# Attention inside a fused AdaLN-attention-MoE kernel: values stationary, row sums on VectorE, softmax in halves, paired merges, first loads reordered

## The reference

```python
# _L0_cond_ref: one 256x256 matrix and bias for each sequence, picked by its category
c = einsum('bsi,bij->bsj', x, weight[ids]) + bias[ids][:, None, :]
# _L0_attn_ref: 16 heads of 16; every projection is W plus a low-rank product
Q, K, V = lora_linear(c, ...)
scores = einsum('bqhd,bkhd->bhqk', Q, K) / sqrt(16) + slopes * rel
out = einsum('bhqk,bkhd->bqhd', softmax(scores, axis=-1), V)
x = x + (c + rezero * lora_linear(out, Wo, bo, Ao, Bo))
# _L0_cond2_ref: low-rank product by language; _L0_ffn_ref: a shared GEGLU layer and
# 12 experts, of which each token takes two, weighted by a softmax over their two logits
x = x + shared(xf) + routed(xf)
```

## Time and profile before

| | us |
|---|---|
| median of 3 runs (range) | 844.94 (844.64 to 846.51) |
| profiled execution | 845.6 |
| its span, first to last instruction | 843.5 |
| PE busy / VectorE busy / ScalarE busy / GpSimd busy | 811.8 / 546.8 / 282.0 / 406.1 |
| granted TensorE clock, mean | 0.992 |

### The profile page before, as it was taken

The page is one execution under the profiler, slowest core; times in us unless marked ns, Lnnn a source line. Parts: engine busy times, 40 slices in busy tenths (PEclk is TensorE's granted clock), DMA queues, the critical chain, the costliest instruction groups (busy, mean ns, idle before and its releaser), DMA issues. The chain is left out here.

```text
span 843.5 us, 27449 instructions
## 1 busy us (share of the span) xinstructions
PE 811.8 (96%) x9371; PEld 675.0 (80%) x9372; DVE 546.8 (65%) x1231; ACT 282.0 (33%) x783; POOL 406.1 (48%) x511
## 2 busy tenths in 40 slices
PE   6899999999999999979999999999999999999995
PEld 5778888888888888856777888888888888888884
DVE  2586666666666667758887567676676666666662
ACT  0333333333333333433332333232323333332330
POOL 2133333444334444210101277777777777777762
PEclk9999999999999999999999999999999999999998
DMA  9445555555555553103863323222232323232222
GB/s 277 130 137 173 171 161 156 157 167 156 160 168 154 153 158 90 46 2 139 251 209 125 125 34 39 35 35 37 33 39 32 39 33 39 33 38 34 35 34 25
DMA packets 49004, 85.59 MB, mean 101 GB/s; under 512 B 7266, under 2 KB 27554, under 8 KB 48834
## 3 DMA queue, kind: packets, MB, share of 16 engines
q1 hardware_dynamic: 33634, 68.76, 26.2%
q0 software_dynamic: 13888, 15.13, 13.4%
q10 hardware_dynamic: 1440, 1.16, 0.5%
HBM read 68.48 MB, written 16.55 MB: 101 GB/s over the span
## 5 line engine op out<-in xcount | busy, mean ns | idle before, releaser
L1429 PE MATMUL ps<-arena,stage 128*128 x900 | 206.6, 379 | 0.0
L1429 PEld LDWEIGHTS ps<-arena,stage 128*128 128x128 f32 x900 | 165.3, 190 | 19.4
L480 POOL DMA_INDIRECT out_dram<-stage,to_row x75 | 120.6, 1608 | 74.9 <-DVE stage L1040 63.4
L636 ACT ACTIVATE stage<-ps 128x384 f32<-128x384 f32 x150 | 65.4, 488 | 241.6 <-PE ps L1416 241.6
L1416 PE MATMUL ps<-token_rows,token_rows_T 64*128 64x128 f32 x1800 | 129.2, 272 | 0.0
L1416 PEld LDWEIGHTS ps<-token_rows,token_rows_T 64*128 64x128 f32 x1800 | 118.8, 189 | 1.7
L472 POOL DMA_INDIRECT token_rows<-gated_rows,from_row x75 | 75.0, 1000 | 64.6 <-DVE to_row L923 42.0
L388 POOL TENSOR_TENSOR arena<-arena 128x256 f32<-128x256 f32 x32 | 23.3, 729 | 148.7 <-DVE arena L764 148.7
L1014 DVE COPY token_rows<-ps 128x128 f32<-128x128 f32 x75 | 21.8, 291 | 109.6 <-PE ps L1398 109.6
L1024 DVE TENSOR_TENSOR stage<-ps,stage 128x384 f32<-128x384 f32 x150 | 75.8, 547 | 1.8 <-ACT stage L636 1.8
L735 DVE TENSOR_REDUCE arena<-ps 128x16 f32<-128x1024 f32 x32 | 39.2, 1224 | 49.4 <-PE ps L1167 49.2
(11 more groups left out here) (170 smaller groups left out, 1482.1 us busy)
## 6 DMA issues: line engine op xcount, KB each, us to landing
stage<-in_we_dram SPq DMA_DIRECT2D x36, 512.0 KB, 4.2
arena<-in_cond_w_dram SPq DMA_DIRECT2D x64, 256.0 KB, 2.9
arena<-in_we_dram SPq DMA_DIRECT2D x12, 768.0 KB, 4.9
arena<-in_x_both_dram SPq DMA_DIRECT2D x32, 256.0 KB, 2.6
arena<-in_L_cond_bias_dram SPq DMA_DIRECT2D x64, 64.0 KB, 2.7
out_dram<-arena SPq DMA_DIRECT2D x32, 128.0 KB, 1.7
be_bc<-in_be_rows_dram SPq DMA_DIRECT2D x13, 192.0 KB, 2.7
gated_rows<-token_rows POOLq DMA_DIRECT2D x2, 1152.0 KB, 10.2
```

The lines of the kernel that those rows point to most:

```text
L480: pool.indirect_dma_start(out_rows, bass.IndirectOffsetOnAxis(to_row[:, t:t + 1], 0), y_sb[t % YR], None, compute_op=ALU.add).then_inc(d_a ...
L636: nc.scalar.activation(g_sb[hf].rearrange("p (j n) -> p j n", n=P), first_out[1][:, :, hf, :], ACT.Gelu).then_inc(g_ok, 1)
L1429: last = mm(ps[:, 4 + s % 2, 0:D], actT_sb[s % 2][:, hf, j * P:(j + 1) * P], arena[:, ds(e * E2 + (NJ * hf + j) * D, D)], start=(hf == 0 a ...
```

## The change

- `attend`: V is stationary (`vD` of 32 columns, without ones) and the transposed probabilities move, 64 columns. Each product lands in one of four column groups (32 partitions) of bank 7, already transposed: head dimension on partitions, queries along the row. It comes after `condition`, and in a tile with a merge between its weights and its biases.
- The row sums are a VectorE reduction over the 1024 probabilities (`sums`), inverted by `invert`, spread to 16 columns a head by ScalarE (`inverse_wide`), transposed by PE in the next tile (`inverse_transpose`), copied by ScalarE (`invT_copy`). `normalize(i-1)`, one multiplication, stands between the halves of `shift(i)`. The score no longer waits for `o_sb`.
- `shift` and the exponential work on halves of 512 columns, and the first four transposes of probabilities wait for the first half alone.
- Merges 0 and 1 of an expert run together at the end of the odd tile (`merge_pair`): weights fill bank 6, biases go to bank 7. ScalarE copies the biases at once (`pair_bias_copy`) and the weights in the next tile (`pair_copy`, 512 columns). In that next tile `low_rank` comes after the projections, and PE waits for `pair_bias` before `inverse_transpose`. SyncE loads stages 0 and 1 after one wait. The waits on merge counts are renumbered.
- First loads: x of tile 0 in two halves, `consts` in two parts (identity and `kmask` first), `ali_f` on SyncE's queue, the other constants behind, awaited under three semaphores; both category values are read before the four condition loads; tile 1 is loaded before Wo. The projection order becomes K, Q, V, O. VectorE adds c and the weights before the language constants, which move into tile 0 (`lang_setup`) and behind it; `router_rows` moves into tile 0, `router_products` behind it, and eight warm matmuls stand after `condition(0)`.

The core of the diff (removed lines are those of the kernel above):

```diff
+        near_loads = [(bo_bc, a["bo_rows"]), (bv_half, a["bv_half"])]
+        rest_loads = [
+            (ba[:, :, :].rearrange("p c n -> p (c n)"), a["lora_ba"]), (consts[:, EARLY:], a["consts"][:, EARLY:]),
+            (lang_i[:, :], a["lang_of"]), (lang_b[:, :], a["lang_rows"]),
+            (a_rows, a["lora_a"]), (aT.rearrange("p c l n -> p (c l n)"), a["lora_aT"])]
+        FIRST, NEAR, REST = 16 * 2, 16 * (len(near_loads) + 1), 16 * len(rest_loads)
+        PROJECTIONS = (1, 0, 2, 3)
...
+            sp.dma_start(x_in[0][:, D:2 * D], a["x_both"][0, :, D:2 * D]).then_inc(d_x[0], 16)
+            sp.dma_start(wm[PROJECTIONS[0]].rearrange("p c n -> p (c n)"), a["wT"][PROJECTIONS[0]]
+                         ).then_inc(d_wT[PROJECTIONS[0]], 16)
             sp.wait_ge(d_cat, 16)
             load_condition(0, 0)
...
             def exps(i):
...
+                for half in range(2):
+                    act.wait_ge(shift_sb, 2 * i + (half + 1))
+                    part = probs[:, 512 * half:512 * half + 512]
+                    nc.scalar.activation(part, part, ACT.Exp).then_inc(prob_sb, 1)
...
+            def inverse_wide(i):
+                act.wait_ge(inv_sb, i + 1)
+                if not isinstance(i, int) or i > 0:
+                    act.wait_ge(invT_ps, i)
+                for m in range(KC):
+                    heads = inverse.rearrange("p (g m h) -> p m g h", m=KC, h=2)[:, m]
+                    last = copy(inv_wide[:, m * P:(m + 1) * P].rearrange("p (g h d) -> p g h d", h=2, d=HD),
+                                heads.unsqueeze(3).to_broadcast([P, 4, 2, HD]))
+                last.then_inc(wide_sb, 1)
+            def invT_copy(i):
+                act.wait_ge(invT_ps, i + 1)
+                if not isinstance(i, int) or i > 0:
+                    act.wait_ge(o_sb, i)
+                copy(inv_T, ps[:, 7, D:2 * D]).then_inc(invT_sb, 1)
...
                 if not isinstance(i, int) or i > 0:
                     dve.wait_ge(pT_ps, 2 * i)
...
+                    dve.wait_ge(rsum_sb, i)
+                for half in range(2):
+                    banks = slice(2 * half, 2 * half + 2)
+                    top = smax[:, 8 * half:8 * half + 8].rearrange("p (g h) -> p g h", g=2)
+                    V.tensor_reduce(top, scores[:, banks], AX.X, ALU.max).then_inc(max_sb, 1)
+                    dve.wait_ge(max_sb, 2 * i + (half + 1))
+                    V.tensor_tensor(probs[:, 512 * half:512 * half + 512].rearrange("p (g h k) -> p g h k", g=2, k=S),
+                                    scores[:, banks], top.unsqueeze(3).to_broadcast([P, 2, 4, S]),
+                                    ALU.subtract).then_inc(shift_sb, 1)
...
+            def sums(i):
+                dve.wait_ge(prob_sb, 2 * i + 2)
+                if not isinstance(i, int) or i > 0:
+                    dve.wait_ge(inv_sb, i)
+                V.tensor_reduce(rsum, probs.rearrange("p (a k) -> p a k", k=S), AX.X, ALU.add).then_inc(rsum_sb, 1)
+            def invert(i):
+                dve.wait_ge(rsum_sb, i + 1)
+                if not isinstance(i, int) or i > 0:
+                    dve.wait_ge(wide_sb, i)
+                V.reciprocal(inverse, rsum).then_inc(inv_sb, 1)
             def normalize(i):
                 dve.wait_ge(o_ps, i + 1)
...
+                dve.wait_ge(invT_sb, i + 1)
+                if not isinstance(i, int) or i > 0:
+                    dve.wait_ge(att_ps, i)
+                V.tensor_tensor(oT.rearrange("p c n -> p (c n)"), ps[:, 7, 0:D], inv_T, ALU.mult).then_inc(o_sb, 1)
...
+            def lang_setup():
+                low_rank_weight(3, PROJECTIONS[3])
+                dve.wait_ge(d_rest, REST)
+                V.tensor_copy(tri_b[:, :], col["tri"]).then_inc(s_const, 1)
+                V.tensor_copy(lang_tmp, lang_b[:, :])
+                link(V.tensor_copy(lang_f, lang_i[:, :]))
+                for lang in range(NLANG):
+                    ins = V.tensor_scalar(lang_hot[:, :, lang], lang_f, float(lang), None, ALU.is_equal)
+                ins.then_inc(s_hot, 1)
+                dve.wait_ge(s_hot, 1)
+                lang_routers()
+            def tile_steps(i, odd, between=lambda: None):
                 shift(i)
                 if one_more:
                     k_spread(i + 1)
+                between()
                 if not isinstance(i, int) or i > 1:
                     t_mask(i - 2)
                 if not isinstance(i, int) or i > 0:
                     x2_add(i - 1, not odd)
                 pT_copy(i)
+                sums(i)
                 if one_more:
                     v_spread(i + 1, not odd)
+                invert(i)
                 if not isinstance(i, int) or i > 1:
                     logit_sum(i - 2)
...
                 if two_more:
                     c_add(i + 2, odd)
+            low_rank_weight(0, PROJECTIONS[0])
             c_add(0, False)
...
+            low_rank_weight(1, PROJECTIONS[1])
+            dve.wait_ge(d_first, FIRST)
+            V.tensor_scalar(bq_quarter, bq_col, 0.25, None, ALU.mult).then_inc(s_first, 1)
             k_spread(0)
+            low_rank_weight(2, PROJECTIONS[2])
+            dve.wait_ge(d_near, NEAR)
+            V.tensor_copy(ali, ali_f).then_inc(s_const, 1)
+            V.tensor_scalar(bo_rz, bo_bc, rz, None, ALU.mult).then_inc(s_first, 1)
+            dve.wait_ge(s_zero, 3)
             v_spread(0, False)
             c_add(1, True)
...
+            tile_steps(0, False, lang_setup)
             router_consts()
+            link(V.tensor_scalar(lang_tmp, lang_tmp, col["lang_row"], col["one_row"], ALU.is_equal, ALU.add))
+            for hf in range(2):
+                V.tensor_scalar(langB[:, hf, :], lang_tmp, col["half"][:, hf:hf + 1], None, ALU.mult)
...
             def prob_transpose(i):
...
+                    if n % 4 == 0:
+                        pe.wait_ge(prob_sb, 2 * i + (n // 4 + 1))
...
             def attend(i, odd):
...
+                if not isinstance(i, int) or i > 0:
+                    pe.wait_ge(x2T_sb, i)
+                for m in range(KC):
+                    for b in range(2):
+                        for g in range(4):
+                            last = mm(ps[32 * g:32 * g + 32, 7, m * P + b * S:m * P + (b + 1) * S],
+                                      vD[int(odd)][:, b, 4 * m + g, :], probsT[:, 2 * g + m, b * S:(b + 1) * S],
                                       start=True, stop=True)
                 last.then_inc(o_ps, 1)
...
+            def inverse_transpose(i):
+                pe.wait_ge(wide_sb, i + 1)
+                for c in range(KC):
+                    last = tr(ps[:, 7, D + c * P:D + (c + 1) * P], inv_wide[:, c * P:(c + 1) * P], ident)
+                last.then_inc(invT_ps, 1)
+            def output(i):
                 pe.wait_ge(o_sb, i + 1)
...
             def merge(n, j, arrived, rows, inside):
...
+                merge_weights(j, 0)
+                inside()
+                merge_biases(j, 6, CW).then_inc(merge_ps, 1)
+            def merge_pair(e, i, inside):
+                for j in range(2):
+                    pe.wait_ge(d_stage[j], 16 * e + 32)
+                pe.wait_ge(tT_sb, i - 1)
+                pe.wait_ge(merge_sb, 2 * e + 2)
+                pe.wait_ge(x2T_sb, i)
+                for j in range(2):
+                    merge_weights(j, j * CW)
+                inside()
+                for j in range(2):
+                    last = merge_biases(j, 7, D + j * P)
...
+            def tile_steps(i, odd, merged, single=None, pair=None, after_pair=None,
+                           between=lambda: None):
...
                 score(i)
                 if one_more:
                     c_transpose(i + 1)
...
+                if after_pair is not None:
+                    pe.wait_ge(pair_bias, after_pair + 1)
+                if not isinstance(i, int) or i > 0:
+                    inverse_transpose(i - 1)
+                if late and after_pair is None:
                     low_rank(i - 2, merged)
                 if one_more:
                     project_k(i + 1)
                     project_q(i + 1)
...
+                if late and after_pair is not None:
                     low_rank(i - 2, merged)
+                between()
                 if not isinstance(i, int) or i > 0:
                     output(i - 1)
                 prob_transpose(i)
...
                     x2_transpose(i - 1, not odd)
                 if one_more:
                     project_v(i + 1)
...
                 if two_more:
                     condition(i + 2, odd)
...
+                if single:
+                    merge(*single, rows=i - 1 if late else None, inside=lambda: attend(i, odd))
+                elif pair is not None:
+                    merge_pair(pair, i, inside=lambda: attend(i, odd))
+                else:
+                    attend(i, odd)
             condition(0, False)
+            warm(8)
+            pe.wait_ge(d_first, FIRST)
             c_transpose(0)
```

(35 more changed lines are left out.)

209 lines of the change are left out of this document (74 added, 135 removed).

## The result

The changed kernel takes **825.2 us** (median; 824.58 to 825.74) against 845.04 of the kernel before on the same chip: a ratio of 0.9758, 95% interval 0.9743 to 0.9773. One further execution took 2746.6 us and is left out; nothing here explains it. The profiled execution took 824.58, with a span of 822.7 (before 843.5) and a mean clock of 0.994.

What follows compares the result with a forecast made beforehand. TensorE was taken to bound the attention stage, VectorE's softmax close behind. From 845.6 us: start -6.3, merge pairs -7.1, tiles 27 to 29 -0.4, tile 30 -0.8, tile 3 +0.9 gave 831.9, as a median 831; range 820 to 842.

Steps and rivals of the forecast that it cites:

- The start: Loads and setup before tile 1: first score at 18.0 to 18.5 us against 25.83, 6.3 us gained after tile 0's payback.
- Attend: Its 32 passes in each tile would take 0.60 us instead of 0.99, saving 0.38 a tile (0.2 to 0.48).
- The chain to x2: VectorE's operations up to `x2_add`: TensorE would newly idle 0.44 us before the x2 transposes, starting at T + 5.84.
- Of the halves nothing is left: Softmax halves: x2 transposes would still come 0.2 us later than before in merge tiles, 0.3 later in the others.
- Even and odd tile: Merge tiles: even 10.32 us against 10.50, odd 11.40 against 11.81, 0.59 a pair, times 12: 7.1 us.
- Late tiles: Tiles 27 to 29, after the merges: 8.9 us each against 9.05, 0.4 us gained in all.
- Tile 30: The tile without condition, after the late tiles: 0.8 us gained.
- Tile 3: TensorE waits for `logit_consts` on VectorE there; the merge that lay in that hole is gone: 0.9 us lost.
- Pairing: Both merges at the odd tile's end: the second merge counted as 1.28 us within the odd tile's 11.40.
- Rival (a): TensorE does not wait for x2, as the halves overlap better: 17 us at most, 820 us; chance 20%.
- Rival (c): Attend's column groups do not run together: 1.86 us an attend, 1.26 more in 32 tiles, 871 us; chance 5%.

Runs made afterwards that it cites:

- e1: Kernel before with only the new start (load order, projection order, setup work, warm matmuls): 838.06 us, ratio 0.9904.
- e9: Changed kernel with attend's loop order turned, all passes of column group 0 first, then 1, 2 and 3: 843.3 us.
- e3: Changed kernel with maximum, subtraction and exponential over all 1024 columns at once, normalisation between maximum and subtraction: 832.19 us.
- e11: Changed kernel with tiles 3 and 4 ahead of TensorE's loop and 44 warm matmuls before tile 3's K projection: 823.7 us.
- e4: Changed kernel with the merges one by one as before the change, in bank 6 alone: 820.68 us.
- e2: Changed kernel with attend, normalisation and output as before: probabilities stationary, V moving, normalisation after attend: 835.04 us.
- e5: Changed kernel with the logit constants in small pieces, ahead of the loop and in each turn, instead of one block: 820.12 us.
- e10: Changed kernel with single merges and the logit constants in small pieces, low-rank rows still transposed before x2: 819.49 us.
- e6: Changed kernel with the matmuls of attend issued twice: 836.16 us.
- e7: Changed kernel without row sums, VectorE reducing a constant of 128 ones a partition instead of the 1024 probabilities: 822.13 us.
- e12: Changed kernel with the logit constants in small pieces and x2 added, transposed and copied ahead of the low-rank rows: 817.81 us.
- e8: Changed kernel with single merges, logit constants in small pieces, and x2 added, transposed and copied ahead of the low-rank rows: 818.44 us.

## Why the prediction was right, and where its terms were not

The forecast of 831 had the right sign, the right sources and the right bottleneck, and 825.2 lies in its range. It fell 6 us short, and the sum of the terms hides larger errors on both sides: by the table, 2.1 us too little at the start, 4.4 in the pairs and 2.6 at the end, against 2.0 too little lost in tile 3. That these partly cancel is luck.

- **The start** (-6.3 predicted). Score 0 at 18.0 to 18.5: it came at 18.21, with the clock at 1.0 from 17 to 24 us. The part that tile 0 pays back was taken about right: I had tile 1 at 28.8, e1 has it at 28.35, and the whole change, whose tile 0 is shorter, at 26.99. The -8.4 at score 3 are e1's 6.6 and 1.8 that the rest of the change brings in tiles 0 to 2, for which I had nothing.
- **Attend, the mis-sized term.** I took 0.60 us with bounds of 0.51 and 0.77; it takes 0.41, below both. The bounds came from weight loads that kept the loader busy 16 and 24 ns a pass. e9 shows what I had not seen: the rate depends on whether neighbouring matmuls go to different column groups, 13 ns a pass if so and 36 if not. In the sum the 0.19 us too much in 32 tiles is 6 us, but in the pairs other terms that I had too short take most of it back. A pair came out 0.39 below the forecast; 0.26 of that lies before the x2 transposes and 0.13 behind them, where attend stands. In the even tile `condition` took 0.76 us instead of 0.70 there, and the step from the bias merge to the score 0.86 instead of 0.78. The rule that I weighed from the Trainium skill's page TensorEngine Tiling (Array Packing), Instruction Overhead, about 60 cycles a matmul, would have made it 0.80 as an estimate over passes, and the trace disagrees. Counted over the 16 matmuls instead it gives an estimate of 0.40, close to the 0.41; but e9 has the same 16 matmuls in 1.15, so the rule alone does not tell the two orders apart.
- **The chain to x2.** The new wait is where I put it, released by `x2_add`, but is 0.19 us instead of 0.44 in odd tiles and 0.15 in late ones, and even tiles don't have it. The 0.25 before the second four transposes of the probabilities is 0.12 to 0.19 in odd tiles and nothing in even and late ones. The operations behind the second subtraction start where I had them (K spread 4.06 us after the score, I had 4.02); between K spread and `x2_add` I kept the old distance and rounded up, 1.30, and it is 1.09. In the even tile K waits 0.48 us for the copy of cT, as I had it, and that came out of idle time, as I had it too. By the matmuls, as I counted, the x2 transposes start at 5.80 in the even tile, without a wait, at 5.62 in the odd one and at 5.43 in a late one; I had 5.84 for all.
- **"Of the halves nothing is left"** was wrong as a price. It is true against the kernel before; but the halves are what pays for `normalize` in the chain. Without them e3 loses 5.9 us between scores 0 and 31.
- **Even and odd tile**: 10.32 and 11.40 predicted, 10.22 and 11.11 measured. Late tiles 8.9 against 8.33: 0.41 of it is the earlier x2 transposes, the rest stands behind them. Tile 30 gained 1.59 (9.05 to 7.46) where I had 0.8.
- **Tile 3, wrong in size** (0.9 predicted, 2.9 measured). I counted the missing merge with 0.9; its passes behind the wait cost 1.3. I had no term for the clock, which e11 prices at 0.90 us. Together they are the 2.2 by which e4 is shorter there. `normalize` moved into the shift, so the output projection now stands behind the constants too, but the size does not come from that: e2, where the projection doesn't wait, loses as much. The other 0.7 stays open.
- **Pairing** I had inside the 11.40; it costs 0.10 us a pair in the loop and 2.2 us in tile 3 (e4), 3.4 in all. With the constants in pieces it is neutral (e5 against e10).
- **Rival (a)**, 820, is nearest in number but not in mechanism: TensorE does wait for x2. Rival (c), groups not concurrent, was priced at 1.86 us an attend; e9, which makes them so by hand, has 1.15. I had slower from 1.04 on; at 1.15 the kernel is still at 0.9963 of the time before, as the other parts gained more than I had.

The parts, undone one at a time, add to 7.0 + 11.7 + 5.9 - 3.4 = 21.2 against 20.8 of the span. With what e2 and e3 differ behind score 31 (-0.7 and +1.4) it is 21.9. Parts need not add, and either remainder is less than the 2 us by which score 0 scatters; I don't explain it.

## What to carry to other kernels

When small matmuls go to column groups of the array, write the loop so that neighbours go to different groups, and price them by a row of that pattern, not by the loader's busy time of another shape. When work is moved for the steady state, look at the one place where an engine has a long block ahead of it (here 5.4 us of constants) and at what filled the wait behind it: the loop can gain while one tile pays 3 of some 24 us back. Cutting that block into pieces brought 5.1 us, more than undoing the pairing (3.4 us between scores 0 and 31) or the x2 order (1.1 to 2.3). A part that looks worthless against the old schedule can be what makes another part affordable; only undoing each part by itself shows it.

## What the runs showed of the hardware

- 32 passes of 128 rows, 32 stationary and 64 moving columns take 0.41 us round four column groups and 1.15 us group by group.
- After TensorE's weight loader had stood 3.28 us idle, the granted clock was 0.68 and 0.50 in the next two windows of 2 us. After 1.60 us (e4) and 2.15 us (e6) idle, and after the wait filled with 44 matmuls (e11), it stayed at 1.00; after 2.58 (e9) and 2.65 us (e7) it fell to 0.50. In the changed kernel's tile 3 the low clock costs 0.90 us.
- The second VectorE multiplication of 128x768 elements (L818) takes 0.96 us in e11 and 1.42 in the changed kernel. GpSimd's operation on 128x256 beside it (L426) takes 1.43 where L818 takes 0.96, and 0.62 where it takes 1.42; why one or the other is long is not shown.
- The same start reaches score 0 between 16.93 and 18.98 us. The extremes go with the landing of the four weight loads of 256 KB, median 5.7 us in e7 (16.93), 5.8 in e12 (17.14), 6.1 in the changed kernel (18.21) and 6.7 in e6 (18.98). But e9 has 5.7 at 18.06 and e8 6.5 at 18.20, so the landing alone does not account for it; the cause is open:

```profile
arena<-in_wT_dram SPq DMA_DIRECT2D x4, 256.0 KB, 6.1
```
